# A mixture-of-experts stage: loops written out, rows loaded and transposed earlier, one register load per slot

## The reference, cut to what matters

```python
xn = _layernorm(x)                                   # 2048 rows of 512
idx = argmax(xn @ router_w.T)                        # one expert per row
for e in range(8):
    g = bitlinear(xn, wg[e]); u = bitlinear(xn, wu[e])
    y = bitlinear(jnp.square(jax.nn.relu(g)) * u, wd[e])
    out = out + jnp.where((idx == e)[:, None], y, 0.0)
# bitlinear: rows scaled by 127 / max|row| and rounded, weights to -1, 0, 1 times a mean
x = x + tanh(g_ffn[0]) * out
```

## Time and profile before

| | us |
|---|---|
| median of three runs (1764.06 to 1765.05) | 1764.71 |
| profiled execution | 1768.54 |
| its span, first to last instruction | 1766.8 |
| TensorE matmuls busy in the span | 1456.9 |
| VectorE busy | 1261.2 |
| ScalarE busy | 970.0 |
| GpSimd busy | 467.0 |
| mixture phase, first row load to last scaling | 561 to 679 |

### The profile page before, as it was taken

How to read it: one execution, slowest core, us unless ns; L and a number is a source line. 1 busy time by engine, 2 the same in 40 slices (tenths; PEclk the granted TensorE clock), 3 DMA queues, 4 the chain that set the end, 5 groups by cost and what they waited for, 6 DMA issues and landing times. The chain is left out here.

```text
span 1766.8 us, 24778 instructions
## 1 busy us (share of the span) xinstructions
PE 1456.9 (82%) x8465; PEld 838.0 (47%) x8536; DVE 1261.2 (71%) x1517; ACT 970.0 (55%) x1440; POOL 467.0 (26%) x359
## 2 busy tenths in 40 slices
PE   4989988999551774778999989898857599999996
PEld 3454534555240333323555555555433366666663
DVE  4878856655582676849999999999758686655551
ACT  5878733344170555413776767676643386665551
POOL 0222200000223004403555666666852000000000
PEclk9999998999855996877999999999989699999998
DMA  6788750000083126520342423335227386666640
GB/s 221 244 256 285 231 205 2 0 0 0 1 355 111 65 88 175 127 84 10 75 99 65 101 67 93 78 74 152 78 77 233 140 306 220 219 219 220 219 142 28
DMA packets 145955, 236.93 MB, mean 134 GB/s; under 512 B 11336, under 2 KB 61512, under 8 KB 144720
## 3 DMA queue, kind: packets, MB, share of 16 engines
q1 hardware_dynamic: 140368, 210.65, 38.8%
q0 software_dynamic: 5504, 25.20, 3.9%
HBM read 169.74 MB, written 59.59 MB: 130 GB/s over the span
## 5 line engine op out<-in xcount | busy, mean ns | idle before, releaser
L1703 ACT ACTIVATE t_e<-t_psE 128x512 f32<-128x512 f32 x512 | 304.8, 597 | 161.0 <-PE t_psE L1806 152.5
L1741 DVE TENSOR_REDUCE t_nmax<-t_psM 128x1 f32<-128x1024 f32 x256 | 301.7, 1212 | 16.6 <-PE t_psM L1787 16.5
L1639 POOL TENSOR_TENSOR t_low<-t_e 128x1024 bf16<-128x1024 f32 x128 | 244.1, 1908 | 172.6 <-ACT t_e L1703 122.5
L1749 DVE TENSOR_TENSOR t_low<-t_e 128x1024 bf16<-128x1024 f32 x128 | 195.0, 1523 | 23.7 <-ACT t_e L1703 23.4
L1817 PE MATMUL t_psO<-t_e,vst 128*96 128x512 bf16 x512 | 201.4, 393 | 11.0 <-POOL t_low L1639 11.0
L1787 PE MATMUL t_psM<-kst,qst 96*128 96x512 bf16 x512 | 165.1, 407 | 42.7 <-DVE t_nmax L1741 37.5
L1806 PE MATMUL t_psE<-qst,kst 99*128 99x512 bf16 x512 | 196.0, 384 | 0.1
L1817 PE MATMUL t_psO<-t_low,vst 128*96 128x512 bf16 x512 | 193.7, 378 | 0.0
L2273 PE MATMUL e_psG<-prebob,e_w1p 128*128 (+1 forms) x1536 | 171.9, 275 | 12.6 <-DVE e_hT L2217 7.8
L2273 PEld LDWEIGHTS e_psG<-prebob,e_w1p 128*128 128x128 bf16 x1536 | 150.9, 98 | 34.0 <-issue 8.0
L2288 PE MATMUL e_psO<-e_w2p,e_hT 128*128 128x512 bf16 x752 | 164.9, 379 | 0.8
(11 more groups left out here) (233 smaller groups left out, 2327.2 us busy)
## 6 DMA issues: line engine op xcount, KB each, us to landing
piece<-in_L_ffn_w SPq DMA_DIRECT2D x32, 1024.0 KB, 13.7
xres<-in_L_ffn_w SPq DMA_DIRECT2D x32, 1024.0 KB, 14.9
wT<-ternary POOLq DMA_DIRECT2D x8, 1536.0 KB, 21.4
kst<-keys SPq DMA_DIRECT2D x96, 128.0 KB, 4.3
mixed<-t_ost SPq DMA_DIRECT2D x64, 192.0 KB
c_rows<-in_ctx SPq DMA_DIRECT2D x8, 1024.0 KB, 10.0
xres<-in_L_ffn_wg SPq DMA_DIRECT2D x8, 1024.0 KB, 8.1
xres<-in_L_ffn_wu SPq DMA_DIRECT2D x8, 1024.0 KB, 6.0
```

The costliest lines, as they stand in the source:

```text
L1639: nc.gpsimd.tensor_tensor(low[:, slot(h, u), :, :], e32[:, slot(h, u), :, :], upper(h, u), ALU.subtract).then_inc(lo_pool, 1)
L1703: nc.scalar.activation(e32[:, slot(h, u), i, :], psE[:, i, :], ACT.Exp, scale=SC).then_inc(expd, 1)
L1741: nc.vector.tensor_reduce(nmax[:, h // G % 2, h % G, u:u + 1], banks_of(place_of_max(b, m)).rearrange("p a t -> p (a t)"), AX_X, ALU.max, ...
L1749: nc.vector.tensor_tensor(low[:, slot(h, u), :, :], e32[:, slot(h, u), :, :], upper(h, u), ALU.subtract).then_inc(lo_dve, 1)
```

## The change

In `mixture_phase` alone:

- All four programs' loops are replaced by steps written out from 0 to 22.
- SyncE loads two more row slots behind the prefetch (4 and 5), and step j loads row slot j+6 instead of j+4, still ahead of store(j). The ring of four places stays.
- ScalarE's step is h_copy(j), x_copy(j+3), q_casts(j+1), squares(j+2).
- TensorE's step is h_transposes(j), x_transposes(j+3), gate_and_up(j+2), down(j).
- The expert's register is loaded once per slot, in `gate_and_up`, and kept until `down` of that slot.

```diff
@@ sync
                 prefetch(sp)
-                with sp.Fori(0, (NS - 4) // 4) as i:
-                    for k in range(4):
-                        load(4 * i + k + 4, k)
-                        store(4 * i + k, k % 2)
-                for j in range((NS - 4) // 4 * 4, NS):
-                    if j + 4 < NS:
-                        load(j + 4, j % 4)
+                for j in range(4, 6):
+                    load(j, j % 4)
+                for j in range(NS):
+                    if j + 6 < NS:
+                        load(j + 6, (j + 6) % 4)
                     store(j, j % 2)
@@ scalar
                 def step(j, par, left):
                     h_copy(j, par)
+                    if left >= 3:
+                        x_copy(j + 3, 1 - par)
                     if left >= 1:
                         q_casts(j + 1, 1 - par)
                     if left >= 2:
                         squares(j + 2, par)
-                    if left >= 3:
-                        x_copy(j + 3, 1 - par)
@@
-                with act.Fori(0, MAIN // 2) as i:
-                    step(2 * i, 0, 3)
-                    step(2 * i + 1, 1, 3)
-                for j in range(MAIN, NS):
+                for j in range(NS):
                     step(j, j % 2, NS - 1 - j)
@@ vector
-                with dve.Fori(0, (NS - 4) // 4) as i:
-                    for k in range(4):
-                        step(4 * i + k, k % 2, 2, True, k)
-                for j in range((NS - 4) // 4 * 4, NS):
+                for j in range(NS):
                     step(j, j % 2, NS - 1 - j, j + 4 < NS, j % 4)
@@ tensor
+                experts = {}
+
                 def weights_of(j):
-                    e = nc.tensor.value_load(expert_of[0:1, bass.ds(j, 1)], min_val=0, max_val=E - 1)
+                    e = experts[j]
                     return lambda m, k: wT[:, bass.ds(e, 1), m, :, k, :].rearrange("p o r d -> p (o r) d")
 
                 def gate_and_up(j, par):
+                    experts[j] = nc.tensor.value_load(expert_of[0:1, bass.ds(j, 1)], min_val=0, max_val=E - 1)
                     w = weights_of(j)
@@
                 def step(j, par, left, slot3):
                     h_transposes(j, par)
+                    if left >= 3:
+                        x_transposes(j + 3, slot3)
                     if left >= 2:
                         gate_and_up(j + 2, par)
-                    if left >= 3:
-                        x_transposes(j + 3, slot3)
                     down(j, par)
+                    del experts[j]
@@
-                with pe.Fori(0, (NS - 4) // 4) as i:
-                    for k in range(4):
-                        step(4 * i + k, k % 2, 3, (k + 3) % 4)
-                for j in range((NS - 4) // 4 * 4, NS):
+                for j in range(NS):
                     step(j, j % 2, NS - 1 - j, (j + 3) % 4)
```

More of the change, by code:

```diff
@@ L991, in mixture_phase @@
         out_v = mixture_dram.rearrange("(n p) d -> n p d", p=P)
-        MAIN = (NS - 3) // 2 * 2
-        assert NS - 3 == MAIN
         with nc.Block() as block:
```

## The result

| | before | after |
|---|---|---|
| median of 6 runs each, us | 1765.02 (1764.06 to 1769.91) | 1757.34 (1756.44 to 1759.86) |
| ratio after to before, 95% interval | | 0.9951 (0.9937 to 0.9965) |
| span of the first traces, us | 1766.8 | 1758.1 |

By the ratio, the change made the kernel about 8.6 us faster (the two medians differ by 7.7); 5.0 were forecast. On the median of 1764.71 that the forecast started from, the ratio gives 1756.1, just under its range (1757.2 to 1763.6). The first pair of traces differs by 8.7 us as well, but what was to become clear is that not all of this is the change.

A forecast was written before the change was run, and what follows sets the result against it. It took the circle of waits between VectorE and ScalarE to bound the mixture stage. Loops -4.9 and start -0.1, all else 0, sum to -5.0 us, forecasting 1759.7 us; 8 in 10 range 1757.2 to 1763.6.

The forecast's parts named there:

- the circle: Mixture slot: VectorE product, quantised tile, ScalarE cast, relu, square, next product; 4.52 us in the loop, 4.28 in the tail.
- Loops written out: Products 2 to 22: all 20 slots take the written-out tail's 4.28 us, 85.6 in place of 90.5, -4.9 us.
- Rival C: VectorE's loop: only its four turns cost, at most 0.32 us each, gain 1.3, time 1763.4; chance 0.04.
- Loads, transposes, row copy, register load: Mixture slots: rows loaded six ahead, row transposes and row copy moved earlier, one register load fewer; each priced at 0.
- The transposes' slack: TensorE, steady slot: gate and up ends at 2.2 us after a product, relu wants it at 3.01; slack 0.8 us.
- Rivals A and B: TensorE's register load and transposes in series: A 4.53 us per slot, 1764.8, chance 0.08; B 4.84, 1771.0, 0.05.
- The start: Around slot 2, TensorE at 1.2 GHz: moved transposes cost 0.15, VectorE saves 0.24; net -0.1, bounds -0.6 and +0.6.
- Rival D: TensorE's clock at stage starts: a rise one gate and up earlier gives 1.2 to 2.4 us more, about 1757.5; chance 0.10.
- The end: From product 22 on: all waits stay the same through cast, transposes, copy, down and scaling; 0.
- A sign that was misread: ScalarE, steady slots: its idle time before the cast should fall by about 0.6 us per slot.
- The last sign: The unchanged stage behind: the prediction is wrong if it moves by more than 2 us against the mixture's end.

The follow-up runs named there:

- loops_kept: The kernel before with rows loaded six ahead and the new ScalarE and TensorE orders, loops and two register loads per slot kept; ratio 0.9994.
- spread: The changed kernel with gate and up three slots ahead and ScalarE's square ahead of the cast; 1736.07 us, ratio 0.9821.
- old_orders: The changed kernel with the old orders on ScalarE and TensorE; products 1 to 2 in 4.63 us, no whole time given.
- two_loads: The changed kernel with the expert's register loaded twice per slot again; products 2 to 22 in 85.61 us, 1 to 2 in 5.76, no whole time given.
- rows_first: The kernel of spread with row transposes ahead of head transposes and row copy ahead of head copy; 1729.97 us, ratio 0.9805.
- vector_only: The kernel before with VectorE's loop alone written out; ratio 0.9974, 4.6 us.
- warm_into: The changed kernel with 133 extra unused matmuls behind the router's last and 8 at the head of TensorE's mixture program; 1759.3 us.

## Why the prediction was right, and where it was not

- **What bounds the kernel, the circle.** Right, and shown from both sides: loops_kept removes TensorE's wait and gains nothing, spread opens the circle and takes 19.6 us more off the stage than the change does.
- **Loops written out, -4.9.** Right: -4.86 in the first pair, -4.5 as a mean of four and four (the 0.5 us row wait was in one trace of before only, so the six-ahead loads are worth about nothing). VectorE alone brings 4.2. Rival C (only the turns of the loop cost, gain 1.3) is out: slots without a turn take 4.51 to 4.62 us against 4.28, those with one 4.64 to 4.65, and the gain is 4.5. The Trainium skill's price for a branch (Advanced Engine Details and Errata, Control Flow Timing) is the price of a turn and so not that of the loop form here; between 0.02 and 0.14 us is what a turn adds to a slot by these traces.
- **Loads, transposes, row copy, register load, each 0.** Right for the steady slots, by loops_kept, old_orders (85.61) and two_loads (85.61). The transposes' slack was 1.2 us where I had 0.8.
- **Rivals A and B** (TensorE the bound) were far off; the sum of its durations, 4.0 of 4.28, overstated it. The real slot of TensorE is at most 3.23 us (rows_first).
- **The start, -0.1.** This is the step of the sum that failed, the term that was mis-sized: -1.65 from product 1 to 2 and +0.5 ahead of it, so -1.2. It took TensorE to be at 1.2 GHz at slot 2 after the change as before it. Gate and up of slot 2 took 3.05 to 3.12 us in the four traces of before and 1.90 in the four of after, 1.2 of the 1.65; of the other 0.45 the prediction had VectorE's 0.24. Rival D had the right size (1.2 us per gate and up) but its mechanism, an earlier rise, was wrong: a fall didn't come. The +0.5 ahead of product 1 goes with the rise and not with the kernel: the two traces of before in which the clock rose at 4.9 and 5.0 us after the first transposes have 9.5 us, the other six, of both kernels, in which it rose at 7.3 to 8.0, have 10.0 to 10.4.
- **The end, 0**: +0.25, and this goes with the clock too. In the two traces of before with 11.1 and 11.0 us the clock stayed at 2.4 GHz until 4.8 and 4.9 us after product 22, in the other six until 2.5 to 3.2 us after it. **The first row load, 0**: -0.4, one trace.
- **A sign that was misread.** ScalarE's idle time before the cast was to fall by 0.6 us per slot. It is 1.54 us in the tail of before and 1.54 after the change: in the old order the row copy already stood between the square and the cast (square 658.40, row copy 658.93, head copy 659.40, cast 661.53 in the trace before), so it only changed places with the head copy. The price of 0 holds all the same. The last sign, the stage behind, held at its start (the +0.25 above); all that follows the first gather took 3.5 us more after than before in the first pair, 1.3 as a mean of four and four.
- **Sum**: forecast -5.0, the stage's traces -5.8.
- **The range failed** because it was made from the forecast and the rivals' times alone ("must reach down into D and up toward A and C"), around a median of three times within 1 us, with nothing in it for the scatter of the kernel. Later runs of the same program span 1755.7 to 1775.8, and a comparison with the kernel before has an interval of 2.5 to 5.7 us to either side.
- **What stays open**: the three timings of the changed kernel give -8.6, -7.8 and -9.2 us, the stage -5.8. Two of the three intervals end at -6.2 and -5.8. The spans of four and four traces differ by 5.7 us on average, which would leave nothing over, but one program's spans scatter by more than that. No trace shows 3 us outside of the stage, and none of the runs rules them out. With the stage's -5.8 alone the time would be 1758.9, inside the range; so it is these 2.8 us, whose cause is not known, that put the measured time under it.

## What to carry to other kernels

Follow the circle of waits once around in one slot before pricing an edit: a 15 us wait on the matrix engine was worth nothing, and swapping two instructions in ScalarE's order, with work moved one slot earlier to allow it, took 19.6 us more off the stage, over three times what the whole change took. Where a stretch of the same stage is already written in the form that a change will give the rest, its slot is the best price to be had. And when a change touches a tenth of a kernel, measure that stage in several traces: whole times scattered by twice what was to be measured, while the steady part repeated within 0.05 us, one row wait apart.

## What the runs showed of the hardware

- In this kernel, VectorE's loop with its values in registers cost 0.23 to 0.34 us per slot of eight instructions (4.51 to 4.62 against 4.28) with no turn of the loop in it, and 4.64 to 4.65 with one. The same form on ScalarE, TensorE and SyncE together cost nothing in 19 of 20 slots (4.27 to 4.29 in vector_only). Which of the values in registers costs the time was not tried.
- After 6.3 us without work TensorE was back at 1.2 GHz. In the stage's start, with its gaps, the clock rose between 4.9 and 8.4 us after the first transposes, and in 8 of the 17 traces without warm_into fell again for 3.4 us. Products 1 to 2 took 5.76 to 6.82 us in these, against 4.63 to 4.85 in the six that stayed and have the old circle. The four that rose before 6 us all fell, of the 13 others four.
- Eight 512-column matmuls that the profile gives as 1.90 us occupied TensorE for 1.74, and four with 1.03 for 0.86, so a sum of durations overstates a busy TensorE.
